# Graph scores with half of their chunks as split, rounded products, and the bias adds moved behind the attention weights

## The reference, cut to what matters

```python
self_feat = concat(v, q) @ W_self.T + b_self              # 512x512 per batch
for d in range(2):
    cond = A.sum(-1); vb = A @ w_bias + b_bias            # A: 512 x 20 x 11
    qh = self_feat @ Wq[d].T + bq[d]; kh = kv @ Wk[d].T + bk[d]       # kv = first 20 rows
    aff = einsum('bnhd,bmhd->bnhm', qh, kh) / sqrt(dh)    # 16 heads x 20 keys
    w = softmax(where(cond > 0, aff, NEG) + vb)
    output += einsum('bnhf,hgf->bnhg', w @ kv, Wout[d]) + bout[d]
x = v + relu(output)
```

## Time and profile before

| | before |
|---|---|
| median of 3 runs | 1278.88 us |
| profiled execution | 1278.12 us, span 1276.3 us |
| PE busy | 1213.1 us, 95% of the span |
| VectorE busy | 877.7 us, 69% |
| GpSimd busy | 887.2 us, 70% |
| ScalarE busy | 630.8 us, 49% |
| score products (L1088) | 140.3 us busy, 512 records for 256 float32 products |
| granted TensorE clock, mean | 0.979 of full |

### The profile page before, as it was taken

One profiled execution on the slowest core, in us unless ns is written; L12 is line 12 of the kernel. 1 busy time (PEld: TensorE's weight loads), 2 busy tenths in 40 slices (PEclk: granted clock), 3 DMA queues, 4 the chain that ended last, 5 costly groups with the idle time before them and its releaser, 6 DMA issues.

```text
span 1276.3 us, 18294 instructions
## 1 busy us (share of the span) xinstructions
PE 1213.1 (95%) x6052; PEld 825.6 (65%) x6052; DVE 877.7 (69%) x1444; ACT 630.8 (49%) x1104; POOL 887.2 (70%) x565
## 2 busy tenths in 40 slices
PE   8989999999999879999999999999999999999984
PEld 5347777777777656566666666666576666666542
DVE  2445778778878765756776776676676776777755
ACT  1323453555355445455555465465465465455461
POOL 1115477776867755766887887888798798798734
PEclk9989999999999899899999999999999999999998
DMA  9984256436445465424534534534534534534411
GB/s 335 344 299 148 35 215 223 176 137 245 155 166 187 159 206 151 132 59 108 147 87 112 147 91 108 150 87 107 148 86 107 157 84 110 155 80 115 115 36 58
DMA packets 111134, 184.03 MB, mean 144 GB/s; under 512 B 39376, under 2 KB 50960, under 8 KB 105792
## 3 DMA queue, kind: packets, MB, share of 16 engines
q1 hardware_dynamic: 103824, 167.24, 42.9%
q10 hardware_dynamic: 7216, 15.62, 4.0%
HBM read 83.92 MB, written 48.01 MB: 103 GB/s over the span
## 4 chain that ended last, share of the span: by engine, by line
PE 56%; DVE 2%; SPq 1%; issue 1%; DMA 1%; ACT 0%; POOL 0%; DVEq 0%; ACTq 0%; POOLq 0%
PE a_bank L1801 10%; PE a_bank L1850 9%; PE a_bank L1814 9%; PE a_bank L107 9%; PE a_bank L108 8%; PE a_bank L109 8%; PE a_bank L1861 2%; SPq L1314 1%; DMA sk_stack<-kl 1%; DVE keep L1666 1%; DVE rden L1684 1%; PE a_bank L1844 1%; PE a_bank L1825 1%; DVE stat L1705 0%; ACT pt L1562 0%
## 5 line engine op out<-in xcount | busy, mean ns | idle before, releaser
L1666 DVE TENSOR_REDUCE keep<-a_bank 128x1 f32<-128x512 f32 x496 | 330.6, 672 | 226.2 <-PE a_bank L1814 225.1
L1562 ACT ACTIVATE pt<-a_bank 128x512 f32<-128x512 f32 x512 | 304.5, 598 | 348.0 <-PE a_bank L1801 325.8
L1411 POOL TENSOR_TENSOR acc<-acc,pt 128x1024 f32<-128x1024 f32 x120 | 286.9, 2391 | 16.6 <-ACT pt L1562 8.1
L1801 PE MATMUL a_bank<-sq_stack,sk_stack 98*128 98x512 f32 x512 | 217.6, 425 | 9.8 <-issue 8.0
L1814 PE MATMUL a_bank<-sk_stack,sq_stack 96*128 96x512 f32 x496 | 202.2, 408 | 2.4 <-DVE keep L1666 1.8
L1406 POOL TENSOR_TENSOR acc<-pt 128x1024 f32<-128x1024 f32 x60 | 143.6, 2393 | 74.4 <-PE a_bank L1861 50.6
L1801 PEld LDWEIGHTS a_bank<-sq_stack,sk_stack 98*128 98x128 f32 x512 | 97.4, 190 | 94.0 <-issue 66.2
L1088 PE MATMUL g_bank<-m,sf 128*128 128x320 f32 x512 | 140.3, 432 | 1.5 <-ACT g_bank L772 1.5
L1684 DVE RECIPROCAL rden<-a_bank 128x128 f32<-128x128 f32 x128 | 120.4, 943 | 19.5 <-PE a_bank L1844 19.5
L1850 PE MATMUL a_bank<-pt,v 128*32 128x512 f32 x1024 | 124.3, 604 | 0.0
L1088 PEld LDWEIGHTS g_bank<-m,sf 128*128 128x128 f32 x512 | 96.6, 190 | 40.7 <-issue 1.9
(11 more groups left out here) (203 smaller groups left out, 2411.1 us busy)
## 6 DMA issues: line engine op xcount, KB each, us to landing
sq_stack<-qh SPq DMA_DIRECT2D x256, 64.0 KB, 2.0
sk_stack<-kh SPq DMA_DIRECT2D x256, 64.0 KB, 2.0
m<-m_rows SPq DMA_DIRECT2D x8, 1600.0 KB, 6.8
xraw<-in_x_t SPq DMA_DIRECT2D x8, 1024.0 KB, 8.9
xn<-in_x SPq DMA_DIRECT2D x8, 1024.0 KB, 5.5
t_rows<-houth SPq DMA_DIRECT2D x8, 1024.0 KB, 3.9
t_rows<-houtl SPq DMA_DIRECT2D x8, 1024.0 KB, 6.7
hh<-t_rows SPq DMA_DIRECT2D x32, 256.0 KB, 3.7
```

The source lines that it names most:

```text
L1411: nc.gpsimd.tensor_tensor(acc[:, two, :], acc[:, two, :], pt[:, step + 1, two, :], ALU.add).then_inc(s["sum_done"], 1)
L1562: nc.scalar.activation(pt[:, i, 2 * half + k, :], bank[:, k, :], ACT.Exp).then_inc(s["exp_done"], 1)
L1666: nc.vector.reduce_max(mx[:, half, k, n:n + 1], bank[:, 2 + e % 2, :], AX).then_inc(s["emax_done"], 1)
L1801: nc.tensor.matmul(bank[:, k, :], sk[c % 2][0:3 * DH + 2, j, i * P:(i + 1) * P], sq[c % 2][0:3 * DH + 2, j, :], start=True, stop=True).the ...
```

## The change

Of the four weight chunks of m, the first two (`SPL = 2`) are split into `mh` (ScalarE, `hi_m`) and `ml` (GpSimd, `lo_m`), and the same two chunks of the self features into `sfh` and `sfl` (both VectorE, `split_sf`). In each score tile the two other chunks stay float32 products, and each of the split ones becomes three rounded products. `split_sf(b+1)` stands in VectorE's `attention(b)` before the first and the third weight tile (`AT_SPLIT`). PE waits for all four parts before a batch's first score tile. In GpSimd's step `lo_m(b)` comes first.

Beside it: in GpSimd's softmax the four `add_bp` stand together behind the last weight multiply; the back-transposes of all but the last batch use four banks and wait no more for the residual; `store_h` moves in ScalarE's step behind the second weight copy; `WARM` is 4; the load of `bq_rep` moves from ScalarE's queue to SP's, behind the first `wk`; in the attention stage SP issues the last `load_t` behind the stacks; two pairs of semaphores are merged to one each (`adjf_done` and `adjw_done`, `sum_done` and `rc_done`), with the same waits.

```diff
+    place("mh", [P, SPL, 2, HK], F32R, "stack0")
+    place("ml", [P, SPL, 2, HK], F32R, "stack0", 4 * SPARE)
+    for k, name in enumerate(("sfh", "sfl")):
+        place(name, [P, SPL, N], F32R, "stack0", 4 * (2 * HK * SPL + N * SPL * k))
...
-        WARM = 6
+        WARM = 4
...
             sp.dma_start(wk[:, 0], d["wk_t"][0].rearrange("(c p) o -> p c o", p=P)).then_inc(s["ld_wk0"], 16)
+            sp.dma_start(bq_rep[:, :, :, :], d["bq_rep"]).then_inc(s["bq_in"], 16)
...
-            act.dma_start(bq_rep[:, :, :, :], d["bq_rep"]).then_inc(s["bq_in"], 16)
...
+        def back_bank(b, i):
+
+            return 6 + i % 2 if isinstance(b, int) and b == B - 1 else (6, 7, 0, 1)[i]
...
-                        pool.wait_ge(s["rc_done"], 4 * b + i - 1)
+                        pool.wait_ge(s["rc_step"], 2 * (4 * b + i - 1))
                         pool.wait_ge(s["exp_done"], 4 * b + i - 1)
                         v = by_head(i - 2)
                         nc.gpsimd.tensor_tensor(v, v, keys(rc[:, i - 2]), ALU.mult).then_inc(s["w_done"], 1)
-                        if has_former and not last:
-                            add_bp(b - 1, i - 2)
+                if has_former and not last:
+                    for i in range(NT):
+                        add_bp(b - 1, i)
...
+            def lo_m(b):
+
+                pool.wait_ge(s["m_split"], 2 * b + 1)
+                nc.gpsimd.tensor_tensor(ml[:, :, :, :], m[:, 0:SPL, :, :], mh[:, :, :, :].bitcast(F32), ALU.subtract).then_inc(s["m_split"], 1)
+
             def step(b, par, last):
+                lo_m(b)
                 if not last:
                     front(b + 1)
...
             label_products(0)
             label_products(1)
+            lo_m(0)
             softmax(0, False)
...
-                    if o == FC - 1 and not (isinstance(b, int) and b < 2):
-                        store_h(b - 2)
...
+            def hi_m(b):
+
+                act.wait_ge(s["m_in"], 16 * b + 16)
+                nc.scalar.activation(mh[:, :, :, :], m[:, 0:SPL, :, :], ACT.Copy).then_inc(s["m_split"], 1)
...
             def step(b, par, last):
+                hi_m(b)
                 self_features(b, par)
                 for i in range(TILES):
                     hi_weights(b - 1, i)
+                    if i == 1 and not (isinstance(b, int) and b < 2):
+                        store_h(b - 2)
...
             self_features(0, 0)
+            hi_m(0)
             bias_in(0, 0)
...
+            def split_sf(b, par, f):
+
+                dve.wait_ge(s["sf_done"], 4 * b + f + 1)
+                nc.vector.tensor_copy(sfh[:, f, :], sf2[:, par, f, :]).then_inc(s["split_done"], 1)
+                dve.wait_ge(s["split_done"], 2 * SPL * b + 2 * f + 1)
+                nc.vector.tensor_tensor(sfl[:, f, :], sf2[:, par, f, :], sfh[:, f, :].bitcast(F32),
+                                        ALU.subtract).then_inc(s["split_done"], 1)
 
             def attention(b, par):
+                more = not (isinstance(b, int) and b == B - 1)
                 dve.wait_ge(s["sf_done"], 4 * b + 4)
                 dve.wait_ge(s["back_ready"], 4 * b)
                 for i in range(TILES + 1):
+                    if more and i in AT_SPLIT:
+                        split_sf(b + 1, 1 - par, AT_SPLIT.index(i))
...
-                    nc.vector.scalar_tensor_tensor(xn[:, i, :], bank[:, 6 + i % 2, :], 0.0, xn[:, i, :],
+                    nc.vector.scalar_tensor_tensor(xn[:, i, :], bank[:, back_bank(b, i), :], 0.0, xn[:, i, :],
...
+            dve.wait_ge(s["m_in"], 16)
+            for f in range(SPL):
+                split_sf(0, 0, f)
...
+                    pe.wait_ge(s["m_split"], 2 * b + 2)
+                    pe.wait_ge(s["split_done"], 2 * SPL * b + 2 * SPL)
                 for i in range(first, end):
                     pe.wait_ge(s["pre_done"], 4 * b + i + 1)
                     for dr in range(2):
                         out = bank[:, 2 + 2 * (i % 2) + dr, 0:HK]
-                        for f in range(FC):
-                            last = nc.tensor.matmul(out, sf2[:, par, f, i * P:(i + 1) * P], m[:, f, dr, :],
-                                                    start=False, stop=f == FC - 1, skip_group_check=True)
+                        for f in range(SPL, FC):
+                            nc.tensor.matmul(out, sf2[:, par, f, i * P:(i + 1) * P], m[:, f, dr, :],
+                                             start=False, stop=False, skip_group_check=True)
+                        for f in range(SPL):
+                            r = slice(i * P, (i + 1) * P)
+                            nc.tensor.matmul(out, sfl[:, f, r], mh[:, f, dr, :],
+                                             start=False, stop=False, skip_group_check=True)
+                            nc.tensor.matmul(out, sfh[:, f, r], ml[:, f, dr, :],
+                                             start=False, stop=False, skip_group_check=True)
+                            last = nc.tensor.matmul(out, sfh[:, f, r], mh[:, f, dr, :],
+                                                    start=False, stop=f == SPL - 1, skip_group_check=True)
...
-                    if i >= 2:
+                    if i >= 2 and isinstance(b, int) and b == B - 1:
                         pe.wait_ge(s["h_done"], 4 * b + i - 1)
                     for f in range(FC):
-                        last = nc.tensor.transpose(bank[:, 6 + i % 2, f * P:(f + 1) * P],
+                        last = nc.tensor.transpose(bank[:, back_bank(b, i), f * P:(f + 1) * P],
...
+                    if c < 2 or more:
+                        stacks(*ahead(b, c, 2), 0, (1,))
+                    if c < 3 or more:
+                        shift_lo(*ahead(b, c, 1), 0)
                     if c == 1 and more:
                         load_t(b + 1, FC - 1)
                     elif c == 1:
                         load_last(b)
-                    if c < 2 or more:
-                        stacks(*ahead(b, c, 2), 0, (1,))
-                    if c < 3 or more:
-                        shift_lo(*ahead(b, c, 1), 0)
```

More of the change, by code:

```diff
@@ L60 @@
 STK = 16 * 6
+SPL = 2
+AT_SPLIT = (0, 2)
 SPARE = 2 * B * HK - 2 * HK
@@ L455, in graph @@
         m = sb("m", [P, FC + 1, 2, HK])
+        assert nc.sbuf_base == at["stack0"] + 4 * (SPARE + 2 * (FC + 1) * HK)
+        mh, ml, sfh, sfl = (t[n] for n in ("mh", "ml", "sfh", "sfl"))
         z = sb("z", [P, N], F32R)
@@ L481, in graph @@
         SFB = (6, 7, 0, 1)
-        s = sems(nc, ctx, "x_in m_in v_in gb_in set_up bits_set pre_done rs_ready z_done adjf_done adjw_done nmr_done sf_ready "
-                          "sf_done adj_step sc_ready mult_done add_done mx_done sub_done exp_done sum_done "
-                          "rc_done w_done wtr_ready wh_done wl_done att_mm att_done back_ready h_done "
+        s = sems(nc, ctx, "x_in m_in m_split split_done v_in gb_in set_up bits_set pre_done rs_ready z_done adjw_step nmr_done sf_ready "
+                          "sf_done adj_step sc_ready mult_done add_done mx_done sub_done exp_done rc_step "
+                          "w_done wtr_ready wh_done wl_done att_mm att_done back_ready h_done "
                           "st_done mv_done ve_done rstd_done ln_done lnt_ready lnt_done bp_in hb_done hh_done hl_done")
@@ L649, in label_products @@
             def label_products(b):
-                pool.wait_ge(s["adjf_done"], b + 1)
+                pool.wait_ge(s["adjw_step"], 2 * b + 1)
                 nc.gpsimd.tensor_tensor(adjw[:, :, :], adjw[:, :, :], t["wbias"][:, :].unsqueeze(1).broadcast_to(
-                    [P, NT * 2 * NK, L]), ALU.mult).then_inc(s["adjw_done"], 1)
+                    [P, NT * 2 * NK, L]), ALU.mult).then_inc(s["adjw_step"], 1)
             def softmax(b, has_former, last=False):
@@ L777, in labels_float @@
                 act.wait_ge(s["adj_step"], 5 * b)
-                nc.scalar.activation(adjw[:, :, :], adj[:, :, :], ACT.Copy).then_inc(s["adjf_done"], 1)
+                nc.scalar.activation(adjw[:, :, :], adj[:, :, :], ACT.Copy).then_inc(s["adjw_step"], 1)
             def exps(b):
@@ L920, in labels @@
                 dve.wait_ge(s["add_done"], 4 * b)
-                dve.wait_ge(s["adjw_done"], b + 1)
+                dve.wait_ge(s["adjw_step"], 2 * b + 2)
                 nc.vector.tensor_reduce(vb[:].rearrange(flat), adjw[:, :, :], AX, ALU.add).then_inc(s["adj_step"], 1)
@@ L953, in softmax @@
                         dve.wait_ge(s["exp_done"], 4 * b + i - 1)
-                        nc.vector.tensor_reduce(sm[:, i - 2], v, AX, ALU.add).then_inc(s["sum_done"], 1)
-                        dve.wait_ge(s["sum_done"], 4 * b + i - 1)
-                        nc.vector.reciprocal(rc[:, i - 2], sm[:, i - 2]).then_inc(s["rc_done"], 1)
+                        nc.vector.tensor_reduce(sm[:, i - 2], v, AX, ALU.add).then_inc(s["rc_step"], 1)
+                        dve.wait_ge(s["rc_step"], 2 * (4 * b + i - 1) - 1)
```

(4 more changed lines are left out.)

## The result

| | before | after |
|---|---|---|
| median | 1278.93 us (1277.53 to 1282.53, 4 runs) | 1320.74 us (1319.78 to 1321.38, 4 runs) |
| profiled execution's span | 1276.3 us | 1319.4 us |
| granted TensorE clock, mean | 0.979 | 0.960 |
| first to second T0 and on, a step | 44.02 us | 51.1 us |
| attention stage begins | 478.05 us | 532.97 us |

What follows compares the result with a forecast made beforehand. PE was taken to bound the graph step (busy 42.8 of 44.0 us), with VectorE only 1.5 us behind. Terms 12.4 + 35.4 - 0.7 = 47.1 us gave 1278.9 + 46 = 1325 us, range 1288 to 1336.

Steps and rivals of the forecast that it cites:

- start, to the first T0 behind the first step, net of the 0.7: First batch and step (T0: first score tile's end): later first product, clock, splits, 12.4 us; prologue wins 0.7.
- six steps: Graph steps 2 to 7, each 5.9 us longer including the clock's 1.0, together 35.4 us.
- last batch: From its first tile on nothing changes, since its weights wait for VectorE and GpSimd.
- attention stage: SP issues 8 loads of transposed rows a few us later there; taken 0, bounds -1 and 2.
- the long step: Graph step with four adds behind the weights: 48.9 us instead of 44.0, before the clock's 1.0.
- The ladder: Softmax end: each exclusive VectorE instruction waits out GpSimd's next; first attention product at 36.75 instead of 32.0; chance 0.50.
- The rival with one rung less: `cadd` is free of GpSimd, or one VectorE instruction keeps its turn: step +3.3 us, 1312 us in all; chance 0.22.
- The rival without exclusion: The new VectorE and GpSimd instructions do not exclude each other; splits cost 1.1 us each, 1283 us in all; chance 0.09.
- the second split: Ahead of the third low part: its copy waits 1.2 us, PE's third group starts at 40.3 instead of 35.0.
- I take 1.0: PE's lower clock behind its wait for the first attention product: 1.0 us a step, at most 2.2, at least nothing.
- The price of a product: Score tiles: a rounded 320-column product costs 0.145 us (0.105 to 0.227), so a tile falls from 4.30 to 3.89.
- The rival in which PE alone decides: Graph steps gain all that PE saves: 1269 us, or 1258 if the order at the start costs nothing; chance 0.07.

Runs made afterwards that it cites:

- e2: Kernel before the change, with only the four bias adds moved behind the weights and `store_h` moved with them; 1280.6 us, ratio 1.001.
- e6: Changed kernel, with the high parts of the split self features written by ScalarE from PSUM instead of copied by VectorE; 1290.7 us, ratio 1.009.
- e10: Changed kernel, with GpSimd's subtraction of m behind the low parts of x instead of ahead of them; 1308.8 us, ratio 1.021.
- e5: Changed kernel, with 24 unused rounded products filling PE's wait in five of the six long steps; 1309.7 us, ratio 1.023.
- e1: Kernel before the change, with only the attention stage's last load of transposed rows issued behind the key stacks; 1270.0 us, ratio 0.992.
- e7: Changed kernel, with GpSimd's first subtraction of m ahead of the label multiply of batch 1; 1314.8 us, ratio 1.026.
- e11: Changed kernel reworked: split high parts by ScalarE, low parts by GpSimd, m's subtraction later, adds among the weights, batch 0 unsplit; 1263.0 us, ratio 0.987.
- e3: Changed kernel, with the four bias adds put back between the weight multiplies; 1314.4 us, ratio 1.026.

## Why the prediction was right, and where its terms were off

**By its own sum** (12.4 + 35.4 - 0.7 = 47.1 us of span; measured 43.1):

| term | forecast | measured |
|---|---|---|
| start, to the first T0 behind the first step, net of the 0.7 | 11.7 | 12.1 |
| six steps | 35.4 | 41.5 |
| last batch | 0 | 1.35 |
| attention stage | 0 (-1 to 2) | -11.8 |

The forecast of the median was 4 us too long, and that it is as near as this is luck: the steps, the start and the last batch together cost 7.8 us more than forecast, and the attention stage gave back 11.8. The mechanism of the long step was the one forecast.

**The ladder held, rung by rung.** In us after T0, forecast and measured ends: mask 28.2 and 28.76; `blocked` 29.5 and 30.0; `cadd` 31.0 and 31.3; the copy 32.5 and 32.7; the subtraction 35.95 and 36.0; first product 36.75 and 36.78. The rival with one rung less fell with `cadd` at 1.28 us, in after and alone in e2. The rival without exclusion fell with the split's 1.48 and 3.26 us, and e6 and e10 moved these by the rungs, where that rival would leave them unmoved. The Trainium skill ("SBUF — State Buffer", section "SBUF: two separate sides") has an exclusive lock that VectorE operations with two SBUF inputs take against GpSimd operations that read SBUF, for the whole instruction; the trace agrees, with `cadd` 0.39 us alone and 1.28 beside GpSimd.

PE was ready for that product 31.55 after T0, not 30.4, and so waited 5.23 us and not 6.3. One held VectorE instruction had been left out: `ve` (L1026), in the LayerNorm ahead of the second mask product, ended with a GpSimd instruction, 1.09 us long instead of 0.42, and tile 3 began at 10.93 and not 10.45. The ladder behind it hid that.

**A step is 7.07 us longer, not 5.9.** The two columns of the table of experiments give it: 4.78 to the first product (4.75 forecast), and 2.29 from there on. With the clock kept up (e5) that stretch is 11.55 us, 0.47 shorter than before, which is the tile's 0.4. So the clock costs 2.76, where I had put 1.0 with a bound of 2.2; and the second split costs nothing, where I had put half a microsecond. The mis-sized term is "I take 1.0". The row of the last batch showed 2.2 behind waits of 3.42 and 1.17; in after the wait is 5.23 and the price a little more. The nearest row was the better estimate, and there was no reason to halve it. The bound was too low as well.

**The attention stage was the step that failed.** I costed the moved load at nothing, -1 to 2. It brings 10.5 us of the stage alone (e1). The view that held it was the costliest groups on the page of before: ahead of the stage's products on the stacks PE idled 9.8 us, 8.0 of it "issue", and SP's queue was the only thing in the change that touched this stage. I read "a few us later" for the loads and did not ask what stands behind them in SP's queue: the stacks, for which PE waits.

**The start** came out near its sum: first score product at 111.61, forecast 111.1, or 110.4 with the 0.7 us won in the prologue, of which these two traces show nothing (ScalarE's first eviction of self features is at 96.43 in before and 96.85 in after). From there to the first T0 it cost 1.7 us, forecast 2.4. e7 shows that of the start's sum 6.3 us were order, not work.

**The price of a product** held: rows 360.94 and 361.09 are 0.15 us apart, and the six in a row 0.147, forecast 0.145. The estimate of 136 ns by the Trainium skill ("TensorE: Matmul & The Clock Gate", section "Back-to-back issue gap") is too low by 8%, and its 216 ns for the 512 columns of the earlier trace rows by 5%. The tile fell from 4.30 to 3.9 us. Of this only the first tile's 0.4 counts in a step; what tiles 1 to 3 save, PE waits later: the change sped up the engine that then waited. The rival in which PE alone decides fell, also in e11, where it had its best chance.

**Left open.** The last batch's 1.35 us, and the spread of some us in the attention stage, were not looked into. Whether the low part of m could be had in time on GpSimd is not tried; by the rows of e11 it would bring at most 1.0 us a step. What decides whether the clock falls behind a wait is open too.

## What to carry to other kernels

Before giving an engine a short instruction beside another engine that excludes it, write down what stands next in the other's queue: the instruction costs that, not its own length, and a chain of n such instructions costs n of the other's. Moving the other's work away only lets its next instruction in (e3, 6 us won; e10, 12 us, with a shorter one next); what helps is to give the short instructions to a third engine (e6, 30 us for two copies of 0.43) or to the other engine itself (e11). An engine made faster wins only as far as the next late input: list these first, here VectorE's 1.5 us of room and the bias of tile 3. And look at each queue that a moved DMA passes, whichever stage it is in: there lay nearly all that this change gained.

## What was not expected of the hardware

A wait of 2.20 us ahead of PE's attention was followed once by a granted clock of 1.00 and once by 0.87 over the next stretch, in turns from step to step (e6): the same gap costs 0 or 1.6 us. Behind a longer one, 3.60 us, it was 1.00 (e10), and behind 4.6 to 4.8 us 0.79 to 0.88 (e3): the length of the gap alone does not decide. Behind 5.2 us it was 0.79 or 0.80 over the whole stretch in each of the five steps read in after, and 0.50 (1.2 GHz, the lower of its two levels) over the first 4.8 us of it; products that nobody needs, put into the gap, kept it at 1.00 (e5) for 0.2 us at the first product.
